# Attention with rotary rows: each causal mask one bf16 product over all 128 rows, both scores of a head pair first, in place of two on 64-row halves

## The chip, the cores and the metric

The kernel runs on one core of a Trainium2 chip. The metric is device time in microseconds (us) for one execution. It holds a whole model of four layers in one launch; the change touches one of its stages.

## The reference

Four layers of mixed attention, recurrences and experts follow one another. The stage in question is the attention of layer 3, with compressed keys and values and with rotary parts:

```python
kv_c = x @ W_kv
kv_c = kv_c * rsqrt(mean(kv_c * kv_c) + EPS) * g_kv
q_c = x @ W_q
k = concatenate([heads(kv_c @ W_kdec, 8), rope(heads(x @ W_krope, 32))])   # 16 heads, 40 rows each
q = concatenate([heads(q_c @ W_qdec, 8), rope(heads(q_c @ W_qrope, 32))])
v = heads(kv_c @ W_vdec, 8)
scores = einsum('bhqd,bhkd->bhqk', q, k) * scale
scores = where(causal, scores, -inf)
out = softmax(scores) @ v
return out_of_heads @ W_o
```

## The kernel before

A stage is a block in which each engine has its own instruction stream, with semaphores between them and a barrier at either end; no stage overlaps the next. `rotary_attention` (L666) works on 8 batches of 512 tokens. Queries and keys lie in `qs` and `ks` with tokens along the free axis: a head takes 40 rows (`KEYED`), even heads at rows 0 to 63 and odd ones at rows 64 to 127, so that two heads are two products on the two halves of the matrix array. Row 40 (`ROWS` is 41) holds, for the queries, the negated maximum of the row and, for the keys, ones.

Each batch goes through two passes. First the **maxima**: for head `n` and query tile `qt`, the scores of 128 queries against the keys up to and with that tile, 128 to 512 columns, are made by `side(("max", ...))` at L877, masked, and DVE reduces them at L1026 to a negated maximum per query (`negmax`). Even heads use bank 6 and odd heads bank 7; PE waits for `taken6` or `taken7`, which DVE signals after its reduction, before it writes a bank anew. The maxima are transposed (`turn`, L884) and sent through DRAM into row 40 of `qs`.

Then the **scores**, transposed, keys by queries: `scores(b, u, pair)` at L926 makes two heads of a pair, 41 rows, from 128 to 512 columns (`first(kt)` to 512), in banks 0 to 3, masks the diagonal tile, and ACT takes the exponential at L1004. `values(b, u)` at L942 multiplies by the values with 128 rows and 32 columns, four heads side by side.

The **mask** is added on the matrix engine: the product of an identity with a table of 0 and -1e30 is accumulated on the diagonal tile of 128 x 128 scores. `masked(out, r, kind)` (L860 to L862) does it on the half of the array that the head uses: two bf16 products of 64 rows, `j` 0 and 1, with the identity and the table split by rows into two halves that are both stored on either half of the partitions (`masksb`, 128 x 2 x 3 x 128). `kind` 1 is the mask of the maxima, 2 that of the transposed scores.

The order on PE is written out: first the maxima of batch 0, 32 pairs (`pair_of_maxima`), called the opening stretch here. Then for each batch 16 steps `u`. A step holds the scores of pair 0, a pair of maxima of the next batch, the scores of pair 1, another pair of maxima, the values of step `u - 1`, and, in some steps, extras from `extras(b, u)`: projections of the batch after the next (L886 to L903), transposes (L884), the sums and the context of the batch before (L912) and its output (L915). The last batch has no maxima to make beside it. The f32 products are two instructions each, one after the other.

The two products of a head are independent of those on the other half: in the order of the program, each pair of maxima is product and masks of the even head, then product and masks of the odd head; a pair of scores is both products, then the masks of both.

Of the kernel before, what the change touches and what calls it, by code (L numbers as in the profile page):

```python
# [14 lines left out]
F32 = mybir.dt.float32  # L15
# [650 lines left out]
def rotary_attention(nc, g, w, d):  # L666
# [7 lines left out]
    tensors = {"qs": ([P, 2, HALVES, T], F32), "ks": ([P, 2, HALVES, T], F32), "negmax": ([P, KT, NH], F32), "maxrow": ([GH, 2, T], F32), "vaug": ([P, 2, KT, NH * CELL], F32),  # L674
               "pt": ([P, 2, KT, T], F32), "o": ([P, 2, T], F32), "sel": ([P, 4, P], F32), "sums": ([P, T], F32), "nope": ([P, 2, T], F32), "prod": ([P, 2, 4, T], F32), "rope": ([P, 2, 2, T], F32),
               "wkv": ([P, 32], F32), "gkv": ([32, 1], F32), "wq": ([P, 64], F32), "wkdec": ([32, P], F32), "wqdec": ([64, P], F32), "wvdec": ([32, P], F32), "wkrope": ([P, 4, P], F32),
               "wqrope": ([64, 4, P], F32), "wo": ([P, P], F32), "cos": ([P, T], F32), "sin": ([P, T], F32), "masks": ([P, 2, 3, P], F32), "masksb": ([P, 2, 3, P], BF16),
               "kvc": ([32, 2, T], F32), "kvsq": ([32, T], F32), "qc": ([64, T], F32), "mean32": ([32, P], F32)}
    loads = [("sel", "sel")] + [(a, "L3a_" + a) for a in ("wkv", "gkv", "wq", "wkdec", "wqdec", "wvdec", "wkrope", "wqrope", "wo", "cos", "sin", "masks")]

# [28 lines left out]
    def pair_of_maxima(b, i):  # L709

        return [("max", b, 2 * (i // KT) + r, i % KT) for r in range(2)]
# [39 lines left out]
    with stage(nc, "L3a", tensors, signals) as (block, t, s):  # L751
# [80 lines left out]
        @block.gpsimd  # L832
        def _(pool):
            own = Chain(pool, s["pool"])
            own(pool.memset(t["mean32"][:, :], 1.0 / 32))
            pool.wait_ge(s["loaded"], START + LOADED)
            own(pool.tensor_copy(t["masksb"][:, :, :, :], t["masks"][:, :, :, :]))
            for r in range(2):
                own(pool.memset(t["ks"][64 * r + 32:64 * r + 64, :, :, :], 1.0))
            own(pool.memset(t["vaug"][:, :, :, :], 0.0))  # L840
            cells = t["vaug"][:, :, :, :].rearrange("p e kt (n c) -> p (e kt) n c", c=CELL)
            own(pool.memset(cells[:, :, :, 3 * HD:4 * HD], 1.0), s["pool_ready"], 1)
            for b in range(BATCH):
                for k in range(4):
                    part, half = divmod(k, 2)
                    for ab in range(2):
                        taken(pool, ("rope", b, part, half, ab))

                    pool.wait_ge(s[f"rope_written{k % 2}"], START + (2 * b + k // 2) * 16)
                    prod = t["prod"][:, k % 2, :, :]  # L850
                    pool.tensor_tensor(t["rope"][:, k % 2, 0, :], prod[:, 0, :], prod[:, 3, :], ALU.subtract).then_inc(s["rope_made"], 1)
                    pool.tensor_tensor(t["rope"][:, k % 2, 1, :], prod[:, 2, :], prod[:, 1, :], ALU.add).then_inc(s["rope_made"], 1)

        @block.tensor
        def _(pe):
            pe.wait_ge(s["loaded"], START + LOADED)
            pe.wait_ge(s["pool_ready"], START + 1)

            def masked(out, r, kind):

                for j in range(2):
                    mm = pe.matmul(out, t["masksb"][64 * r:64 * r + 64, j, 0, :], t["masksb"][64 * r:64 * r + 64, j, kind, :], start=False, stop=(j == 1))  # L862
                return mm

            def side(item):

                bank, k = place[item]
                pe.wait_ge(s[f"taken{bank}"], START + k)
                what, b = item[:2]
                out = ps[:, bank, :]  # L870
                tokens = h[:, b * T:(b + 1) * T]
                if what == "max":
                    n, qt = item[2:]
                    if n % GH == 0 and qt == 0:
                        pe.wait_ge(s["second_stacked" if n else "first_stacked"], START + (b + 1) * STACKED)
                    rows = row_tile(n % 2, KEYED)
                    pe.matmul(out[:, 0:(qt + 1) * P], t["qs"][rows, b % 2, n // 2, qt * P:(qt + 1) * P], t["ks"][rows, b % 2, n // 2, 0:(qt + 1) * P], start=True, stop=False)  # L877
                    mm = masked(out[:, qt * P:(qt + 1) * P], n % 2, 1)
                elif what == "turn":
                    k = item[2]  # L880
                    for r in range(2):
                        taken(pe, ("max", b, GH * k + GH - 2 + r, KT - 1))
                    for qt in range(KT):
                        mm = pe.transpose(out[0:GH, qt * P:(qt + 1) * P], t["negmax"][:, qt, GH * k:GH * (k + 1)], g["ident"][:, :])  # L884
                elif what == "kv":
                    mm = pe.matmul(out[0:32, :], t["wkv"][:, :], tokens, start=True, stop=True)  # L886
                elif what == "qc":
                    mm = pe.matmul(out[0:64, :], t["wq"][:, :], tokens, start=True, stop=True)
                elif what == "rms":
                    pe.wait_ge(s["squared"], START + b + 1)  # L890
                    mm = pe.matmul(out, t["mean32"][:, :], t["kvsq"][:, :], start=True, stop=True)
                elif what == "qn":
                    taken(pe, ("qc", b))
                    mm = pe.matmul(out, t["wqdec"][:, :], t["qc"][:, :], start=True, stop=True)
                elif what == "kn":
                    pe.wait_ge(s["scaled"], START + b + 1)
                    mm = pe.matmul(out, t["wkdec"][:, :], t["kvc"][:, b % 2, :], start=True, stop=True)
                elif what == "rope":
                    part, half, ab = item[2:]
                    if part:  # L900
                        mm = pe.matmul(out, t["wqrope"][:, 2 * half + ab, :], t["qc"][:, :], start=True, stop=True)
                    else:
                        mm = pe.matmul(out, t["wkrope"][:, 2 * half + ab, :], tokens, start=True, stop=True)  # L903
                elif what == "v":
                    pe.wait_ge(s["scaled"], START + b + 1)
                    for kt in range(KT):
                        cols = slice(kt * P, (kt + 1) * P)
                        mm = pe.matmul(out[:, cols], t["kvc"][:, b % 2, cols], t["wvdec"][:, :], start=True, stop=True)
                elif what in ("sums", "ctx"):
                    pe.wait_ge(s["o_copied"], START + 2 * b + 2)  # L910
                    for e in range(2):
                        mm = pe.matmul(out, t["sel"][:, (2 if what == "sums" else 0) + e, :], t["o"][:, e, :], start=(e == 0), stop=(e == 1))  # L912
                else:
                    taken(pe, ("ctx", b))
                    mm = pe.matmul(out, t["wo"][:, :], t["sums"][:, :], start=True, stop=True)  # L915
                mm.then_inc(s[f"ready{bank}"], 1)

            def scores(b, u, pair):

                four, kt = divmod(u, KT)  # L920
                step = b * NH + u
                if step:
                    pe.wait_ge(s["exp_ready"], START + 4 * (step - 1) + 2 * pair + 2)
                for r in range(2):
                    rows = row_tile(r, ROWS)
                    pe.matmul(ps[:, 2 * pair + r, first(kt):T], t["ks"][rows, b % 2, 2 * four + pair, kt * P:(kt + 1) * P], t["qs"][rows, b % 2, 2 * four + pair, first(kt):T],  # L926
                              start=True, stop=False)
                for r in range(2):
                    masked(ps[:, 2 * pair + r, kt * P:(kt + 1) * P], r, 2).then_inc(s["turned_ready"], 1)

            def values(b, u):

# [13 lines left out]
            for item in begun(0) + [("v", 0)] + begun(1):  # L946
                side(item)
            for i in range(NH * KT // 2):
                for item in pair_of_maxima(0, i):
                    side(item)  # L950
                if i == NH * KT // 4 - 1:
                    side(("turn", 0, 0))
            for b in range(BATCH):
                for u in range(NH):
                    if u % GH == 0:
                        pe.wait_ge(s["max_stacked"], START + (2 * b + u // GH + 1) * 32)
                    for pair in range(2):
                        scores(b, u, pair)
                        if b + 1 < BATCH:
                            for item in pair_of_maxima(b + 1, 2 * u + pair):  # L960
                                side(item)
                    if u:
                        values(b, u - 1)
                    for item in extras(b, u):
                        side(item)
                values(b, NH - 1)
# [2003 lines left out]
def layout(inp):  # L2970
# [59 lines left out]
    freqs = np.outer(np.arange(T, dtype=np.float32), 1.0 / 10000.0 ** (np.arange(0, 32, 2, dtype=np.float32) / 32))  # L3030
    o["L3a_cos"], o["L3a_sin"] = (np.repeat(f(freqs).T, 8, 0).astype(np.float32) for f in (np.cos, np.sin))
    later = np.where(np.arange(P)[None, :] > np.arange(P)[:, None], -1e30, 0.0)
    rows = np.stack([np.eye(P), later, later.T], 1).reshape(2, 64, 3, P).transpose(1, 0, 2, 3)
    o["L3a_masks"] = np.concatenate([rows, rows]).astype(np.float32)

    sel = np.zeros((P, 4, P), np.float32)
    for n in range(HEADS):
# [100 lines left out]
```

## Time and profile before

| | us |
|---|---|
| median of 3 executions | 9413.75 |
| lowest and highest | 9409.73, 9447.94 |
| the profiled execution | 9411.23 |
| its span, first to last instruction | 9409.6 |
| PE busy over the span | 6565.9 (70%) |
| DVE busy | 4731.6 (50%) |
| ACT busy | 3170.9 (34%) |
| POOL busy | 2124.2 (23%) |
| mean granted TensorE clock | 0.808 |

The page lists the cost of each group of instructions by its line; PE is the multiplication and PEld the loading of weights, which overlaps it. The granted clock is given as a share of 2.4 GHz: 0.50 is 1.2 GHz. Matmul records overlap, since a product starts while the one before is still draining, so what one costs is read from start to start and not from its listed length.

### The profile page before, as it was taken

The numbers are of one execution on the slowest core, as the hardware profiler recorded it, in microseconds if no ns is written. First come the engines' busy times: TensorE is split into PE (matmuls) and PEld (weight loads), VectorE is DVE, ScalarE is ACT, GpSimd is POOL, SyncE is SP. The second block draws the span as 40 slices with busy tenths as digits, with TensorE's granted clock in tenths as the row PEclk, the third lists the DMA queues.
The fourth block names the chain that finished last, engine by engine and source line by source line (L and its number), as shares of the span: only waits on it lengthen the run. The fifth ranks groups of instructions, "written<-read, shape, count | busy, mean of one in ns | idle before, by whom it ended". The sixth has DMA issues, their size and how long they took to land. (4 is left out here: it accounts for less than half of the span.)

```text
span 9409.6 us, 109969 instructions
## 1 busy us (share of the span) xinstructions
PE 6565.9 (70%) x36292; PEld 3470.7 (37%) x36480; DVE 4731.6 (50%) x7361; ACT 3170.9 (34%) x6905; POOL 2124.2 (23%) x2294
## 2 busy tenths in 40 slices
PE   5677665668766787644556999967677666667677
PEld 3666651511244122211112444434244333334343
DVE  4545534356533665677773444444444555444444
ACT  2111023225433354233331122345354333345354
POOL 1222230322133220233341100033142000043241
PEclk7888776768887788877777687889898777788898
DMA  1000010122111110000000322111110000011110
GB/s 39 0 0 0 10 56 2 66 63 63 54 47 63 43 40 14 12 0 0 0 3 12 67 47 46 23 49 37 33 38 20 7 0 0 12 41 33 36 39 26
DMA packets 260733, 267.76 MB, mean 28 GB/s; under 512 B 113312, under 2 KB 190240, under 8 KB 258400
## 3 DMA queue, kind: packets, MB, share of 16 engines
q1 hardware_dynamic: 250080, 241.23, 9.9%
q0 software_dynamic: 10240, 21.25, 0.7%
q8 instruction: 231, 3.78, 0.2%
q14 instruction: 182, 1.49, 0.1%
HBM read 123.56 MB, written 71.66 MB: 21 GB/s over the span
## 5 line engine op out<-in xcount | busy, mean ns | idle before, releaser
L2036 PE MATMUL ps<-s_l2b_hc,ident 128*128 128x512 f32 x512 | 354.3, 830 | 403.2 <-DVE s_l2b_hc L2128 402.7
L2003 POOL TENSOR_TENSOR s_l2b_Bx<-s_l2b_du,s_l2b_B 128x512 f32<-128x512 f32 x256 | 409.8, 1624 | 620.5 <-DVE s_l2b_du L2116 375.1
L1869 DVE TENSOR_REDUCE s_l3l_negmax<-ps 128x4 f32<-128x512 f32 x256 | 175.0, 683 | 743.6 <-PE ps L1710 743.6
L1710 PE MATMUL ps<-s_l3l_qk 64*64 64x64 f32 (+1 forms) x5632 | 297.6, 255 | 289.6 <-DMA s_l3l_qk<-s_l3l_rope 270.6
L2123 DVE TENSOR_TENSOR_SCAN s_l2b_state<-s_l2b_decay,s_l2b_Bx 128x512 f32<-128x512 f32 x256 | 430.7, 1721 | 109.2 <-POOL s_l2b_Bx L2003 109.2
L1800 ACT ACTIVATE s_l3l_probs<-ps,s_l3l_biases,s_l3l_q_inverse 128x128 f32<-128x128 f32 x1024 | 455.6, 463 | 54.1 <-DVE s_l3l_biases L1871 53.6
L1648 POOL TENSOR_TENSOR s_l3l_probs<-s_l3l_probs,s_l3l_inverse 128x512 f32<-128x512 f32 x256 | 266.7, 1042 | 832.7 <-DVE s_l3l_inverse L1850 832.7
L1672 PE MATMUL ps<-s_l3l_hs,s_l3l_wqk 128*128 128x512 f32 x512 | 301.2, 694 | 195.7 <-DVE s_l3l_prod L1824 100.4
L1026 DVE TENSOR_REDUCE s_L3a_negmax<-ps 128x1 f32<-128x128 f32 (+3 forms) x512 | 236.0, 488 | 350.0 <-PE ps L862 347.7
L602 DVE TENSOR_REDUCE s_L1a_negmax<-ps 128x1 f32<-128x512 f32 x512 | 316.3, 681 | 145.2 <-PE ps L464 144.5
L877 PE MATMUL ps<-s_L3a_ks,s_L3a_qs 40*128 40x256 f32 (+3 forms) x1024 | 354.4, 597 | 31.4 <-DVE s_L3a_kvsq L1041 16.5
L1004 ACT ACTIVATE s_L3a_pt<-ps 128x256 f32<-128x256 f32 (+3 forms) x512 | 195.2, 434 | 516.6 <-PE ps L862 515.0
L602 DVE TENSOR_REDUCE s_L2a_negmax<-ps 128x1 f32<-128x512 f32 x512 | 316.4, 681 | 93.2 <-PE ps L464 92.4
L1794 ACT ACTIVATE s_l3l_turned<-ps 128x512 f32<-128x512 f32 x256 | 153.5, 600 | 533.7 <-PE ps L1718 532.8
L577 ACT ACTIVATE s_L1a_pt<-ps 128x512 f32<-128x512 f32 x512 | 263.0, 602 | 205.4 <-PE ps L500 205.2
L2036 PEld LDWEIGHTS ps<-s_l2b_hc,ident 128*128 128x128 f32 x512 | 121.0, 256 | 570.7 <-DVE s_l2b_hc L2128 346.8
L577 ACT ACTIVATE s_L2a_pt<-ps 128x512 f32<-128x512 f32 x512 | 263.3, 603 | 168.2 <-PE ps L500 168.0
L1606 POOL MEMSET s_l3l_hs<- 64x2 f32 x4 | 0.4, 96 | 1301.2 <-POOLq L42 1301.2
L1710 PEld LDWEIGHTS ps<-s_l3l_qk 64*64 64x64 f32 x5632 | 230.7, 144 | 148.5 <-issue 148.5
L926 PE MATMUL ps<-s_L3a_qs,s_L3a_ks 41*128 41x512 f32 (+3 forms) x1024 | 278.8, 556 | 0.1
L1770 ACT ACTIVATE s_l3l_sq<-ps 128x512 f32<-128x512 f32 x256 | 152.2, 599 | 348.4 <-PE ps L1672 347.7
L1192 PE MATMUL ps<-s_l0a_T,s_l0a_M 128*128 128x128 f32 x1024 | 172.7, 321 | 117.7 <-DVE s_l0a_I L1319 88.4
(673 smaller groups left out, 16026.0 us busy)
## 6 DMA issues: line engine op xcount, KB each, us to landing
s_l3l_qk<-s_l3l_rope SPq DMA_DIRECT2D x1024, 64.0 KB, 2.0
scratch_rope<-s_L3a_rope SPq DMA_DIRECT2D x32, 512.0 KB, 2.8
s_L3a_qs<-scratch_rope SPq DMA_DIRECT2D x64, 128.0 KB
s_L3a_ks<-scratch_rope SPq DMA_DIRECT2D x64, 128.0 KB
s_L0e_slots<-scratch_sent SPq DMA_DIRECT2D x16, 396.0 KB, 6.8
s_L1e_slots<-scratch_sent SPq DMA_DIRECT2D x16, 396.0 KB, 6.2
scratch_square<-s_L1a_rows SPq DMA_DIRECT2D x24, 256.0 KB, 3.1
scratch_parts<-s_L1a_split SPq DMA_DIRECT2D x16, 384.0 KB, 3.1
```

What stands on the lines that cost most here:

```text
L577: act.activation(t["pt"][:, u % 2, j, :], ps[:, j, :], ACT.Exp, scale=scale).then_inc(s["exp_ready"], 1)
L602: taken_by(vec.tensor_reduce(t["negmax"][:, qt, n:n + 1], out, AX.X, ALU.max, negate=True), item)
L877: pe.matmul(out[:, 0:(qt + 1) * P], t["qs"][rows, b % 2, n // 2, qt * P:(qt + 1) * P], t["ks"][rows, b % 2, n // 2, 0:(qt + 1) * P], start ...
L926: pe.matmul(ps[:, 2 * pair + r, first(kt):T], t["ks"][rows, b % 2, 2 * four + pair, kt * P:(kt + 1) * P], t["qs"][rows, b % 2, 2 * four + ...
L1026: taken_by(vec.tensor_reduce(t["negmax"][:, qt, n:n + 1], out[:, 0:(qt + 1) * P], AX.X, ALU.max, negate=True), item)
L1648: own(pool.tensor_tensor(tile, tile, share, ALU.mult), s["probs_ready"], U + 1)
L1672: mm = pe.matmul(out, t["wqk"][:, 2 * e + ab, :], tokens, start=True, stop=True)
L1710: mm = pe.matmul(out[rows, P * k + at:P * k + at + size], t["qk"][rows, b % 2, c, 64 * m:64 * m + 64], t["qk"][rows, b % 2, 4 + c, key:key ...
L1800: act.activation(t["probs"][:, U % (LAG + 1), k, :], ps[:, U % 2, P * k:P * (k + 1)], ACT.Exp, bias=t["biases"][:, U % (LAG + 1), k:k + 1] ...
L2003: pool.tensor_tensor(t["Bx"][:, n % 2, k, :], t["du"][:, k, :], t["B"][:, n % 2, :], ALU.mult).then_inc(s["bx_ready"], 1)
L2036: pe.matmul(ps[:, 4 + k, :], g["ident"][:, :], t["hc"][:, (n - 1) % 2, k, :], start=(n == 1), stop=(n == STATES)).then_inc(s["summed"], 1)
L2123: vec.tensor_tensor_scan(t["state"][:, k, :], t["decay"][:, n % 2, k, :], t["Bx"][:, n % 2, k, :], 0.0, ALU.mult, ALU.add).then_inc(s["sca ...
```

## The change

The table is no longer split: `masksb` is 128 x 3 x 128, with identity and masks over all 128 partitions. `masked` is one bf16 product of 128 rows. The pairs of maxima leave `side` and get a function of their own, `two_maxima`, in which both waits and both products come first and the two masks after them. `scores` keeps its order, with the new masks.

```diff
-"masks": ([P, 2, 3, P], F32), "masksb": ([P, 2, 3, P], BF16),
+"masks": ([P, 3, P], F32), "masksb": ([P, 3, P], BF16),
...
-            own(pool.tensor_copy(t["masksb"][:, :, :, :], t["masks"][:, :, :, :]))
+            own(pool.tensor_copy(t["masksb"][:, :, :], t["masks"][:, :, :]))
...
-            def masked(out, r, kind):
-
-                for j in range(2):
-                    mm = pe.matmul(out, t["masksb"][64 * r:64 * r + 64, j, 0, :], t["masksb"][64 * r:64 * r + 64, j, kind, :], start=False, stop=(j == 1))
-                return mm
+            def masked(out, kind):
+
+                return pe.matmul(out, t["masksb"][:, 0, :], t["masksb"][:, kind, :], start=False, stop=True)
+
+            def two_maxima(b, i):
+
+                pair = pair_of_maxima(b, i)
+                for item in pair:
+                    n, qt = item[2:]
+                    bank, k = place[item]
+                    pe.wait_ge(s[f"taken{bank}"], START + k)
+                    if n % GH == 0 and qt == 0:
+                        pe.wait_ge(s["second_stacked" if n else "first_stacked"], START + (b + 1) * STACKED)
+                    rows = row_tile(n % 2, KEYED)
+                    pe.matmul(ps[:, bank, 0:(qt + 1) * P], t["qs"][rows, b % 2, n // 2, qt * P:(qt + 1) * P], t["ks"][rows, b % 2, n // 2, 0:(qt + 1) * P], start=True, stop=False)
+                for item in pair:
+                    qt, bank = item[3], place[item][0]
+                    masked(ps[:, bank, qt * P:(qt + 1) * P], 1).then_inc(s[f"ready{bank}"], 1)
...
-                    masked(ps[:, 2 * pair + r, kt * P:(kt + 1) * P], r, 2).then_inc(s["turned_ready"], 1)
+                    masked(ps[:, 2 * pair + r, kt * P:(kt + 1) * P], 2).then_inc(s["turned_ready"], 1)
...
-    rows = np.stack([np.eye(P), later, later.T], 1).reshape(2, 64, 3, P).transpose(1, 0, 2, 3)
-    o["L3a_masks"] = np.concatenate([rows, rows]).astype(np.float32)
+    o["L3a_masks"] = np.stack([np.eye(P), later, later.T], 1).astype(np.float32)
```

## Rows read from the trace of the kernel before

**Rows 1.** Busy us by stretch (PE, PEld, DVE, ACT, POOL), granted clock, DMA.

```profile
5215.00:5288.00 73.00, 71.21 (x259) 43.08 (x261) 31.09 (x66) 1.87 (x2) 4.92 (x4) 0.50 0.45 80
5290.00:6077.00 787.00, 752.41 (x5181) 394.85 (x5180) 338.34 (x603) 237.20 (x568) 59.76 (x48) 0.82 0.21 42
```

**Rows 2.** Waits, 5290 to 6036 us: total us, times, longest.

```profile
ACT s_L3a_pt L1004 <- PE ps L862: 497.2, 207, 35.5
...
PEld ps L877 <- DVE s_L3a_negmax L1026: 8.6, 39, 0.4
```

**Rows 3.** Groups by line: count, busy us, mean ns, idle before.

```profile
L862 PE MATMUL ps<-s_L3a_masksb 64*128 64x128 bf16 x2048 | 231.1, 245 | 0.0
...
L1026 DVE TENSOR_REDUCE s_L3a_negmax<-ps 128x1 f32<-128x128 f32 (+3 forms) x512 | 236.0, 488 | 350.0 <-PE ps L862 347.7
```

**Rows 4.** Order of time, 2.4 GHz: start us, length us, engine, line.

```profile
5615.97 0.64 PE L926 MATMUL ps<-s_L3a_qs,s_L3a_ks 41*128 41x512 f32 x1
...
5616.46 0.15 PEld L862 LDWEIGHTS ps<-s_L3a_masksb 64*128 64x128 bf16 x2 [0.19 <-issue]
5616.88 0.27 PE L862 MATMUL ps<-s_L3a_masksb 64*128 64x128 bf16 x3
...
5617.00 0.43 PE L877 MATMUL ps<-s_L3a_ks,s_L3a_qs 40*128 40x256 f32 x1
```

**Rows 5.** Order of time, 1.2 GHz, a pair of 384 columns.

```profile
5598.86 1.65 PE L877 MATMUL ps<-s_L3a_ks,s_L3a_qs 40*128 40x384 f32 x4
...
5599.61 0.21 PEld L862 LDWEIGHTS ps<-s_L3a_masksb 64*128 64x128 bf16 x2 [0.25 <-issue]
...
5600.25 0.48 PE L862 MATMUL ps<-s_L3a_masksb 64*128 64x128 bf16 x4
5600.46 1.01 PE L926 MATMUL ps<-s_L3a_qs,s_L3a_ks 41*128 41x384 f32 x2
```

**Rows 6.** Order of time on PE, 2.4 GHz, where the shape changes.

```profile
6782.54 0.27 PE L1710 MATMUL ps<-s_l3l_qk 64*64 64x128 f32 x1
6782.74 0.33 PE L1718 MATMUL ps<-ident,s_l3l_probs 128*128 128x128 f32 x1
...
5543.38 1.02 PE L912 MATMUL ps<-s_L3a_o,s_L3a_sel 128*128 128x512 f32 x2
...
5543.81 0.59 PE L912 MATMUL ps<-s_L3a_o,s_L3a_sel 128*128 128x512 f32 x1
5544.34 0.59 PE L926 MATMUL ps<-s_L3a_qs,s_L3a_ks 41*128 41x384 f32 x2
```

**Rows 7.** The same at 1.2 GHz.

```profile
6983.83 0.42 PE L1710 MATMUL ps<-s_l3l_qk 64*64 64x128 f32 x1
6984.18 0.47 PE L1718 MATMUL ps<-ident,s_l3l_probs 128*128 128x128 f32 x1
```

**Rows 8.** Weight loads after a change of shape, 512 columns, 2.4 GHz.

```profile
5614.50 0.30 PEld L926 LDWEIGHTS ps<-s_L3a_qs,s_L3a_ks 41*128 41x128 f32 x4 [0.20 <-issue]
5615.04 0.10 PEld L862 LDWEIGHTS ps<-s_L3a_masksb 64*128 64x128 bf16 x2 [0.23 <-issue]
```

**Rows 9.** A batch by stretches: masks (PE, PEld), clock; then all engines, first stretch.

```profile
5416.20:5433.30 17.10, 3.57 (x28) 2.75 (x28) 0.50 0.00 1
5433.30:5477.60 44.30, 11.32 (x106) 7.71 (x106) 1.00 0.12 43
5477.60:5498.10 20.50, 4.99 (x40) 4.06 (x40) 0.50 0.56 92
5498.10:5525.40 27.30, 8.12 (x84) 6.10 (x84) 1.00 0.40 60
...
5416.20:5433.30 17.10, 17.10 (x84) 9.58 (x81) 4.51 (x10) 2.62 (x6) 0.00 (x0) 0.50 0.00 1
```

**Rows 10.** Order of time on PE, where the clock rose and fell.

```profile
5430.33 5.15 PE L912 MATMUL ps<-s_L3a_o,s_L3a_sel 128*128 128x512 f32 x8
...
5524.67 0.95 PE L877 MATMUL ps<-s_L3a_ks,s_L3a_qs 40*128 40x384 f32 x4 [2.76 <-DVE s_L3a_kvsq L1041]
```

More of the change, by code:

```diff
@@ L676, in rotary_attention @@
                "wkv": ([P, 32], F32), "gkv": ([32, 1], F32), "wq": ([P, 64], F32), "wkdec": ([32, P], F32), "wqdec": ([64, P], F32), "wvdec": ([32, P], F32), "wkrope": ([P, 4, P], F32),
-               "wqrope": ([64, 4, P], F32), "wo": ([P, P], F32), "cos": ([P, T], F32), "sin": ([P, T], F32), "masks": ([P, 2, 3, P], F32), "masksb": ([P, 2, 3, P], BF16),
+               "wqrope": ([64, 4, P], F32), "wo": ([P, P], F32), "cos": ([P, T], F32), "sin": ([P, T], F32), "masks": ([P, 3, P], F32), "masksb": ([P, 3, P], BF16),
                "kvc": ([32, 2, T], F32), "kvsq": ([32, T], F32), "qc": ([64, T], F32), "mean32": ([32, P], F32)}
@@ L871, in side @@
                 tokens = h[:, b * T:(b + 1) * T]
[L872 to L879, printed above, removed]
+                if what == "turn":
                     k = item[2]
@@ L948, in _ @@
             for i in range(NH * KT // 2):
-                for item in pair_of_maxima(0, i):
-                    side(item)
+                two_maxima(0, i)
                 if i == NH * KT // 4 - 1:
@@ L959, in _ @@
                         if b + 1 < BATCH:
-                            for item in pair_of_maxima(b + 1, 2 * u + pair):
-                                side(item)
+                            two_maxima(b + 1, 2 * u + pair)
                     if u:
```

## The prediction, made before the changed kernel was run

> **What bounds the kernel now.** The change touches one stage only, the attention with rotary rows, so I first looked for that stage in the view by stretches. Its loop over heads runs from 5215 to 6077 us of the span: the opening stretch of 73 us, which computes only the maxima of batch 0, and then 787 us in which scores, maxima of the next batch and values go round together [rows 1]. PE is listed as busy 752 of the 787 us there. The view of waits says the same from the other side: ACT waits 497 us for the masks of the scores, whereas PE's weight loads for the maxima wait only 8.6 us for DVE's reduction [rows 2]. So the matrix engine sets the time of the stage, and what an edit adds to PE's sequence in the 787 us lengthens the kernel nearly one for one. No other stage starts before this one ends, so nothing gives it back. The opening stretch is different: there each bank's product, masks and reduction form a loop, and a latency counts.
>
> The second thing to read is the granted clock, in the same view: 0.50 in the opening stretch (1.2 GHz throughout) and 0.82 in the 787 us, a mixture of 2.4 and 1.2 GHz [rows 1].
>
> **What a mask costs today.** There are 2048 mask products at L862 [rows 3], four for each pair of heads, in 512 pairs: 256 pairs of scores and 256 of maxima. 32 of the latter are in the opening stretch and 480 pairs in the loop. The order in time at 2.4 GHz reads so: the first pass of a f32 score starts at 5615.97; its second pass starts when the weight load of the mask does, at 5616.46, 0.49 us later (0.43 is the flow of 512 columns, 0.05 a weight load that isn't hidden); the masks start at 5616.88, with no gap; the next score starts at 5617.00, so the two masks hold their half of the array for 0.12 us [rows 4]. The two heads of the pair run side by side, one on rows 0 to 63 and one on 64 to 127, a few hundredths apart, so 0.12 us is the price of all four masks. At 1.2 GHz it is 0.11 for the weight load (0.75 less 0.64 us of 384 columns) and 0.21 for the masks [rows 5].
>
> **The mask products themselves.** After the change two products of 128 rows follow one another. Each is 128 columns long like those of today: 2 x 0.055 = 0.11 us, where two of 64 rows on each half take 0.12. Halving the count from 2048 to 1024 therefore buys nothing on the path: what was done side by side is now done in series. At 1.2 GHz, 2 x 0.107 against 0.21: nothing either. The trace has no bf16 product of 128 rows in this place; from below I take no gain, from above a second mask that waits for a whole weight load of 0.10 instead of 0.055 us, 0.05 x 512 = 23 us. I take nothing, since the masks of today follow one another with the same load between them.
>
> **The change of shape is what costs.** The scores keep 40 or 41 rows on one half of the array, the masks now span both. So PE changes between a half and the whole twice per pair, where it stayed in halves. The trace shows what such a change costs between other lines. From a 64x64 to a 128x128 shape: 0.20 us from the start of a product whose flow takes 0.11, so 0.09 us is lost. From 128x128 back to a half: 5543.81 to 5544.34 is 0.53 us against 0.43 between two passes of the same shape just before, 0.10 lost [rows 6]. At 1.2 GHz: 0.35 against a flow of 0.21, 0.14 lost [rows 7]; I take 0.14 for the way back too, for which no row stands here. The weights of the second pass are hidden worse after a change: 0.54 instead of 0.49 us from the first to the second pass [rows 8]; 0.05 more, and I take the same at 1.2 GHz. Each pair thus pays 0.09 + 0.10 + 0.05 = 0.24 us at 2.4 GHz and 0.14 + 0.14 + 0.05 = 0.33 us at 1.2 GHz. The Trainium skill has the rule in "TensorEngine Tiling (Array Packing)", Key Properties: changing the tiling mode, and not only the tile, drains the engine. It speaks against this change, and by that rule the trace agrees: 0.09 to 0.10 us in each direction, none between equal shapes.
>
> How many pairs run at which clock: in 109.2 us, one batch, 68 of 258 masks fall in the two stretches at 0.50 [rows 9], 26 in 100. Of 480 pairs that is 125 slow and 355 fast: 125 x 0.33 + 355 x 0.24 = 41 + 85 = 126 us.
>
> **The opening stretch.** Both scores now come before either mask, and the masks need the whole array. Today the two banks run their loops apart: product, two masks, own reduction. Now they meet, and the loop from one pair to the next holds both reductions in a row. It gains one reduction, 0.49 us in the mean [rows 3], and a change of shape, 0.14, and loses one mask before the signal, 0.11: 0.52 us x 32 = 17 us. In the loop over heads that serialisation is covered: the next product for these banks comes only after a scores pair or the values, and the values already need both halves of the array.
>
> **Small parts.** The table of masks is half as long, so its load and the cast on GpSimd at the stage's start are shorter. They happen once, and I cost them at nothing. The waits for both banks ahead of the first mask replace waits that stood in the same order; queued behind them on PE are only the masks of the same pair. ACT and DVE get their inputs 0.1 to 0.2 us later, beside idle time that is far larger [rows 2].
>
> Sum at an unchanged clock: 126 + 17 = 143 us.
>
> **The clock.** This is the uncertain term. PE was busy all 17.1 of 17.1 us in a stretch at 0.50, so being occupied isn't what lifts the clock [rows 9]. It rose at 5433.3, while 128x128 products of 512 f32 columns ran, and fell at 5525.4, after a gap of 2.76 us in which PE waited for DVE's reciprocal [rows 10]. The other rise, at 5498.1, came with nothing but scores, maxima and values about, and opened 27.3 us at full clock with 84 masks [rows 9]. That rise looks weak: PE will do the same work there with 0.33 us more of standing per pair. I expect about half of the six such rises to be missed. One missed stretch is 27.3 + 21 x 0.24 = 32 us of work at half the clock, some 27 us more (the waits in it don't stretch): 3 x 27 = 80 us. In the Trainium skill, "TensorE: Matmul & The Clock Gate", Part 1, the clock is set by how busy PE has been. By that rule alone, with PE listed as busy throughout in both kernels, the clock would stay as it is; the first rival below is that case, and the row with 17.1 busy us at 0.50 speaks against reading the rule by listed busy time.
>
> **Forecast.** 143 + 80 = 223 us. The profiled execution took 9411.2 us (span 9409.6), 2.5 under the median of 9413.75, which is no difference here. 9411 + 223 = 9634 us.
>
> **The rivals.**
> - The tax is paid and the clock pattern stays: 9411 + 143 = 9554 us. For it: the gaps that bring the clock down are the same, and 128x128 products come in every batch. Chance 0.25.
> - The tax is paid and the clock is mostly lost in the loop: if half of the remaining 520 us at 2.4 GHz, beyond the 3 stretches, falls to 1.2 GHz, 200 us more or so, 9830 us. For it: every pair of the fast stretches gets thinner too. Against: those with projections of 128 rows in them are dense. Chance 0.12.
> - Nothing moves: the weights of the wide mask are loaded while the scores still flow, and the change of shape is free. Then 0.11 stands for 0.12 us, 9411 us within 10. Against it stand rows 6 and 7. Chance 0.04.
> - Faster: the change of shape is free and products over all 128 rows lift the clock, as they do at 5433. The 787 us at 0.82 hold 283 us at 1.2 GHz; if half of these ran at 2.4 GHz, 70 us would be saved, 9340 us. It decides only where the changes of shape cost less than what the clock gives back, 143 us or 0.14 us per change at most, and the rows put them at 0.09 to 0.14. Chance 0.03.
> - The forecast's own case has 0.56.
>
> Range: low end, the first rival without the weight-load term (0.05 x 512 = 26 us less) and a little better clock, 9535. High end, the forecast with the late second mask (23 us) and four more stretches lost (108 us), 9762, rounded to 9760. That leaves out the faster and the unmoved case and most of the lost clock, 0.2 together. A measurement of this kernel can tell about 0.5%, 47 us, from no change: slower 0.92, same 0.05, faster 0.03.
>
> **What would show it.** In the order of time: masks start 0.09 us after the end of the scores' flow, the next score 0.10 us after the end of the second mask's; 0.54 us between passes at 512 columns. The loop's granted clock under 0.80, with a stretch at 0.50 where 5498 to 5525 was fast. The opening stretch near 90 us in place of 73. The prediction is wrong if the mask's weights are fetched ahead of the change of shape, if PE stops being the bound (ACT's wait for masks would shrink far under 497 us), or if the wide masks count for more in the clock than the narrow ones did.

## The result and the profile after

The changed kernel takes 9589.5 us in the median of 4 executions (9567.8 to 9623.8); the kernel before takes 9421.1 in executions on the same chip. The ratio is 1.0178, with a 95% interval of 1.014 to 1.0216: slower by 168 us. The profiled execution, the shortest of the four, took 9567.8 us with a span of 9566.0, 156 us over the span of before. In all comparisons here two executions are left out in which the chip granted far less clock from start to end: 11514.6 us of the kernel before and 11712.6 us of one of the variants below.

First the view by stretches, the one that says where the time went. Each row gives the stretch, its length, busy us of PE, PEld, DVE, ACT and POOL, the granted clock and the DMA. In this and all such fences the first row is the opening stretch, from the first product of the maxima to the first score, and the second row the loop over heads, to the last score. The kernel before, cut at the same events, then its two last batches (these rows are cut more finely than rows 1):

```profile
5215.10:5287.60 72.50, 70.78 (x259) 42.65 (x260) 30.80 (x64) 1.87 (x2) 4.92 (x4) 0.50 0.45 80
5287.60:6076.90 789.30, 754.71 (x5189) 396.53 (x5187) 339.73 (x605) 237.13 (x567) 59.76 (x48) 0.82 0.21 42
5962.70:6036.60 73.90, 71.53 (x672) 41.59 (x668) 34.77 (x70) 26.14 (x67) 0.00 (x0) 1.00 0.12 17
6036.60:6076.90 40.30, 40.16 (x380) 18.92 (x378) 5.54 (x5) 24.00 (x62) 0.00 (x0) 1.00 0.01 2
```

The changed kernel:

```profile
5200.90:5286.80 85.90, 70.18 (x196) 32.42 (x196) 28.33 (x64) 1.87 (x2) 4.92 (x4) 0.50 0.37 68
5286.80:6235.10 948.30, 919.71 (x4227) 341.99 (x4228) 335.52 (x605) 237.94 (x568) 59.69 (x48) 0.73 0.18 34
6105.20:6189.60 84.40, 82.13 (x542) 34.05 (x538) 33.96 (x69) 26.14 (x67) 0.00 (x0) 1.00 0.10 12
6189.60:6235.10 45.50, 45.45 (x319) 17.27 (x316) 5.93 (x6) 24.81 (x63) 0.00 (x0) 1.00 0.01 2
```

The loop is 159 us longer, the opening stretch 13. The stages ahead came out 12 us shorter in this one execution, which no line of the change explains, and 4 us more went at the start of this stage, where the table of masks is now shorter, and behind it. Of the 159 us, read the clock column: 0.82 became 0.73. A loop of 789.3 us at 0.82 holds 647 us of work at 2.4 GHz, one of 948.3 at 0.73 holds 692. So the work grew by about 45 us, and the time at 1.2 GHz went from 2 x 0.18 x 789 = 284 us to 2 x 0.27 x 948 = 512. This product undercounts the added work: waits and changes of shape in a slow stretch are not twice as long, and more of them now lie in slow stretches. The last two batches ran at 1.00 in both kernels and show the added work with no clock in it: 10.5 us and 5.2 us. Seven batches like the first and one like the second would make 7 x 10.5 + 5.2 = 79 us (an estimate).

Next the order of time on PE in the changed kernel, at 2.4 GHz and then at 1.2 GHz, to be held against rows 4 and 5 (start us, length us, engine, line):

```profile
5710.04 0.28 PE L932 MATMUL ps<-s_L3a_qs,s_L3a_ks 41*128 41x128 f32 x2
5710.25 0.29 PE L861 MATMUL ps<-s_L3a_masksb 128*128 128x128 bf16 x2
5710.46 0.92 PE L873 MATMUL ps<-s_L3a_ks,s_L3a_qs 40*128 40x384 f32 x4
5711.31 0.29 PE L861 MATMUL ps<-s_L3a_masksb 128*128 128x128 bf16 x2
...
5701.33 0.39 PE L861 MATMUL ps<-s_L3a_masksb 128*128 128x128 bf16 x2
5701.40 0.31 PE L861 MATMUL ps<-s_L3a_masksb 128*128 128x128 bf16 x1
5701.65 2.08 PE L873 MATMUL ps<-s_L3a_ks,s_L3a_qs 40*128 40x512 f32 x4
5703.66 0.39 PE L861 MATMUL ps<-s_L3a_masksb 128*128 128x128 bf16 x2
```

The second pass of a score starts at 5710.04 and flows for 0.11 us (128 columns); the masks start at 5710.25, so 0.10 is lost. From the first mask to the next score it is 0.21: two masks one after the other, 0.12, and 0.10 for the way back. From 5710.46 to 5711.31 it is 0.85: two flows of 0.32, 0.11 for the second pass's weights and 0.10 again. At 1.2 GHz it is 0.32 us from the first mask to the next score. The second mask starts at 5701.40 (the row with x1 is the second of the two in the row above it), so 0.25 us lies between its start and the score; its flow takes 0.11, which leaves 0.14 for the change. The 2.01 us from 5701.65 to 5703.66 hold two flows of 0.85, 0.16 for the weights and 0.14 for the change.

The count, as the view of groups has it, against rows 3, and the wait of ACT against rows 2 (here over 5286.8 to 6107 us):

```profile
L861 PE MATMUL ps<-s_L3a_masksb 128*128 128x128 bf16 x1024 | 172.0, 260 | 0.0
...
ACT s_L3a_pt L1008 <- PE ps L861: 586.7, 186, 41.9
```

Half as many masks, as meant. ACT waits longer for PE, so PE is still the bound. And the clock, against rows 9: three of the stretches at 1.2 GHz (masks of PE and PEld, clock) are 44 to 55 us long, where those of rows 9 were 17 and 20. Such a stretch isn't new, since the loop of the kernel before has one of 47.8 us as well; but it has only that one over 40 us, where the changed kernel has four of 44 to 58 us. The last rows show one place of the difference: steps 14 and 15 of a batch and steps 0 and 1 of the next, first in the kernel before (all engines, at full clock and in the one case that it missed wholly), then in the changed one.

```profile
5385.00:5439.60 54.60, 10.65 (x54) 3.55 (x54) 0.50 0.41 59
5531.70:5586.30 54.60, 10.24 (x52) 3.42 (x52) 0.50 0.41 59
5661.40:5705.80 44.40, 7.10 (x36) 2.37 (x36) 0.50 0.30 54
...
5606.20:5625.20 19.00, 18.80 (x173) 10.70 (x170) 8.68 (x19) 6.71 (x17) 0.00 (x0) 0.97 0.53 71
5715.20:5746.10 30.90, 30.90 (x172) 16.17 (x168) 8.63 (x19) 6.71 (x17) 0.00 (x0) 0.54 0.31 44
...
5705.90:5727.20 21.30, 20.97 (x141) 8.27 (x138) 8.58 (x19) 6.71 (x17) 0.00 (x0) 1.00 0.50 63
5553.60:5588.40 34.80, 34.80 (x142) 11.88 (x138) 8.70 (x19) 6.71 (x17) 0.00 (x0) 0.53 0.30 39
```

Of the six passages from one batch to the next that stand in these two traces, the kernel before went through one wholly and one in part at 1.2 GHz; in the changed kernel it was three wholly, at 34 to 36 us each in place of 21.3, and one in part.

### The profile page after: what moved, and what is told of

The parts are those of the page before. It is cut to its first block and busy times, and to the rows that moved or that the text cites. A ratio compares the mean times of both kernels' runs of the same rounds, so it can differ in the third digit from the quotient of the medians.

```text
span 9566.0 us, 107921 instructions
## 1 busy us (share of the span) xinstructions
PE 6717.1 (70%) x35268; PEld 3403.3 (36%) x35456; DVE 4724.2 (49%) x7361; ACT 3171.9 (33%) x6905; POOL 2128.3 (22%) x2294
## 5 line engine op out<-in xcount | busy, mean ns | idle before, releaser
L873 PE MATMUL ps<-s_L3a_ks,s_L3a_qs 40*128 40x128 f32 (+3 forms) x1024 | 340.4, 669 | 36.0 <-DVE s_L3a_kvsq L1045 15.9
```

What stands on the lines that cost most here:

```text
L873: pe.matmul(ps[:, bank, 0:(qt + 1) * P], t["qs"][rows, b % 2, n // 2, qt * P:(qt + 1) * P], t["ks"][rows, b % 2, n // 2, 0:(qt + 1) * P], ...
```

## The experiments

Three questions: is it the change of shape or the new order that costs (A against B); is the lower clock brought by the thinner work on the array (D against E); and can the clock be had back. Ratios are against the kernel before, timed beside them.

**The order alone.** `two_maxima` with the old masks on halves:

```diff
-                    masked(ps[:, bank, qt * P:(qt + 1) * P], 1)...
+                    masked_half(ps[:, bank, qt * P:(qt + 1) * P], item[2] % 2, 1)...
...
-                    masked(ps[:, 2 * pair + r, kt * P:(kt + 1) * P], 2)...
+                    masked_half(ps[:, 2 * pair + r, kt * P:(kt + 1) * P], r, 2)...
```

> The order of the changed kernel (both products of a pair of maxima, then the masks) with the masks of the old one, two products of 64 rows on each head's half. Theory A (changes of shape cost the time): PE never leaves the halves here, so the loop over heads stays at 789 us within 10 and the opening stretch at 72 us; total 9421 us within 25. Theory B (the two heads wait for each other, whatever the mask's shape): the loop keeps over half of the 159 us that the changed kernel added, 870 us or more, total 9500 us or more. The clock of the loop stays at 0.82 by A.

Measured 9443.6 us in the median, ratio 1.0027 (1.0011 to 1.0042). Stretches:

```profile
5224.50:5303.30 78.80, 65.89 (x258) 42.50 (x260) 28.26 (x64) 1.87 (x2) 4.93 (x4) 0.50 0.40 73
5303.30:6123.70 820.40, 778.36 (x5192) 391.07 (x5189) 334.85 (x605) 237.20 (x568) 59.75 (x48) 0.80 0.20 40
```

Theory A is right in the main, since 1.0027 is a small part of 1.0178, but its "unchanged" was wrong. The order costs 6.3 us in the opening stretch, nearly half of the 13.4 there, and in the profiled execution (9455.3 us, 12 over the median) 31 us in the loop, where the clock was 0.80. Theory B's half of the loss is not there.

**Wide masks for the scores alone, and for the maxima alone**, each with masks on halves for the other, whose table is loaded and cast beside the wide one before the opening stretch:

```diff
-                    masked(ps[:, bank, qt * P:(qt + 1) * P], 1)...                    # scores alone
+                    masked_half(ps[:, bank, qt * P:(qt + 1) * P], item[2] % 2, 1)...
...
-                    masked(ps[:, 2 * pair + r, kt * P:(kt + 1) * P], 2)...            # maxima alone
+                    masked_half(ps[:, 2 * pair + r, kt * P:(kt + 1) * P], r, 2)...
```

> Masks of 128 rows for the scores, masks on halves for the maxima (in the new order). Theory A: a step has 6 changes of shape where the old kernel has 2 (into and out of each scores' mask, beside those around the values) and 2 more passes whose weights are exposed: 4 x 0.095 + 2 x 0.05 = 0.48 us per step, 112 steps, plus 0.335 us in the 16 steps of the last batch: 59 us on the loop at 2.4 GHz, some 65 with the part at 1.2 GHz, and up to 40 more if the clock falls; opening stretch unchanged at 72 us. Total 9485 to 9525. Theory B: no change against the old kernel beyond 15 us.

Measured 9594.4 us, ratio 1.0168 (1.0124 to 1.0213).

```profile
5216.40:5295.20 78.80, 65.90 (x258) 42.52 (x260) 28.26 (x64) 1.87 (x2) 4.93 (x4) 0.50 0.38 73
5295.20:6258.80 963.60, 934.45 (x4680) 395.34 (x4677) 335.86 (x605) 237.87 (x568) 59.76 (x48) 0.69 0.18 34
```

> Masks of 128 rows for the maxima, masks on halves for the scores. Theory A: 5 changes of shape per step where the old kernel has 2, one more exposed pass: 3 x 0.095 + 0.05 = 0.335 us x 112 = 38 us on the loop, 45 with the part at 1.2 GHz, none in the last batch, and the opening stretch goes from 72 to 85 us as in the changed kernel. Total 9465 to 9510. Theory B: most of what the changed kernel lost is here, over 100 us, and little in the kernel with wide masks for the scores alone.

Measured 9509.6 us in the median of three executions (9507.5 to 9559.5), ratio 1.012 (1.0072 to 1.0167).

```profile
5210.30:5296.20 85.90, 70.23 (x198) 32.47 (x198) 28.30 (x65) 1.87 (x2) 4.92 (x4) 0.50 0.37 67
5296.20:6182.50 886.30, 850.45 (x4737) 367.46 (x4738) 335.28 (x605) 237.25 (x567) 59.71 (x48) 0.76 0.19 37
```

The opening stretch follows the shape of the maxima's masks, as A said, but from another start: 78.8 us with the order alone and with wide masks for the scores (A had 72), 85.9 with wide masks for the maxima, as in the changed kernel. So its 13.4 us are 6.3 for the order and 7.1 for the shape. The loops miss: both are longer than A's sum, by some 110 and some 50 us, and of the totals that of the wide scores lies outside A's range, while that of the wide maxima is at its upper end. The two halves of the change are not additive either, 1.0168 and 1.012 against 1.0178 together. The clock column shows why. With wide scores alone the loop ran at 0.69, lower than with both, so a loop with less added work (963.6 x 0.69 = 665 us at full clock) took more time. Of its 174 us over the old loop A's count explains some 65, and the rest is left for the clock. So what the clock does isn't a fixed price for each change of shape.

**Fewer changes of shape.** The changed kernel with the masks of a scores pair held back behind the products of the maxima pair:

```diff
                     pe.matmul(ps[:, bank, 0:(qt + 1) * P], t["qs"][...], t["ks"][...], start=True, stop=False)
+                between()
                 for item in pair:
...
-                            two_maxima(b + 1, 2 * u + pair)
+                            two_maxima(b + 1, 2 * u + pair, lambda: score_masks(b, u, pair))
```

> The changed kernel with the masks of a scores pair held back until the two products of the maxima pair behind it are issued, then all four wide masks in a row: 5 changes of shape per step instead of 9, same products and masks. Theory A: 4 x 0.095 + 2 x 0.05 = 0.48 us per step less than the changed kernel, 54 us at 2.4 GHz and about 60 with the slow part, and some of the lost clock back: loop 948 down to 830 to 890 us, clock 0.75 to 0.80, total 9480 to 9545. Theory C (the wide masks themselves hold the array up or draw the clock down, not the changes): the loop stays over 920 us.

Measured 9533.1 us, ratio 1.0118 (1.0089 to 1.0146).

```profile
5231.40:5317.50 86.10, 70.19 (x197) 32.43 (x197) 28.44 (x64) 1.87 (x2) 4.93 (x4) 0.50 0.37 67
5317.50:6211.00 893.50, 851.30 (x4229) 380.38 (x4228) 334.75 (x605) 237.99 (x569) 59.66 (x48) 0.76 0.19 37
```

The same wide masks, 5 changes of shape per step in place of 9: the loop is 55 us shorter (893.5, just over A's 830 to 890), and the clock is 0.76, within what A said. C is out: the wide masks are all there.

**Does density hold the clock?** Three kernels are meant to change only how much dense work there is: the old one with every mask added twice, the changed one with every mask added three times (adding the mask again leaves the result as it is), and the old one without masks, in which the products give the signals that the masks gave, and whose attention isn't causal inside the diagonal tile.

```diff
-                for j in range(2):
+                for j in range(2 * 2):       # halves, twice; j % 2 picks the table
...
-                return pe.matmul(out, ..., start=False, stop=True)
+                for again in range(3):       # wide, three times
+                    mm = pe.matmul(out, ..., start=False, stop=(again == 2))
...
-                    mm = pe.matmul(out, t["masksb"][...], t["masksb"][...], start=False, stop=(j == 1))
+                return None                  # no masks
```

> The old kernel with each mask on a half added twice, eight products per pair where it has four, order and everything else unchanged. It adds 0.115 us per pair at 2.4 GHz, with no change of shape and no gap: 480 x 0.115 = 55 us on the loop over heads (789 us at a clock of 0.82, that is 648 us of work at full clock). Theory D (the clock follows how much of the array is at work, and the masks, which fill both halves with one column per cycle, are dense work): the clock rises to 0.88 or more and the loop comes to (648 + 55) / 0.90 = 780 us, 760 to 815, no longer than before. Theory E (the clock goes its own way and only gaps move it): the clock stays at 0.82 and the loop comes to 855 us or more; total 9490.

Measured 9519.5 us, ratio 1.0101 (1.0075 to 1.0127).

```profile
5310.70:6209.70 899.00, 874.25 (x7107) 473.05 (x7106) 355.91 (x604) 238.83 (x568) 59.67 (x48) 0.86 0.19 37
```

> The changed kernel with each wide mask added three times in a row: 3072 wide products instead of 1024, the changes of shape as many as in the changed kernel. It adds 4 x 0.055 = 0.22 us per pair, 480 x 0.22 = 105 us at full clock to 696 us of such work in the loop. Theory D (dense work lifts the clock): the clock goes from 0.73 to 0.88 or more and the loop to (696 + 105) / 0.90 = 890 us, shorter than the 948 of the changed kernel although it does more. Theory E: the clock stays at 0.73 and the loop is 1050 us or more, total 9690.

Measured 9569.5 us, ratio 1.0165 (1.0143 to 1.0187).

```profile
5301.20:6239.30 938.10, 912.68 (x6145) 433.05 (x6144) 335.52 (x605) 239.04 (x569) 59.68 (x48) 0.86 0.18 35
```

> The old kernel with the masks left out, of the maxima and of the scores, so that attention is not causal inside the diagonal tile; everything else as before. It takes 0.115 us of the densest work from each pair: 55 us off the loop's 648 us of work at full clock. Theory E (the clock doesn't follow the density): clock 0.82, loop 725 us, opening stretch 66, total 9345. Theory D: the clock falls, to 0.70 to 0.76, and eats the gain or more: loop 593 / 0.73 = 810 us, 780 to 850; total 9400 to 9470.

Measured 9420.1 us, ratio 1.0007 (0.9994 to 1.002).

```profile
5283.30:6083.00 799.70, 760.21 (x3271) 330.88 (x3269) 340.89 (x605) 238.73 (x567) 59.75 (x48) 0.72 0.21 41
```

This is the clearest result of the study. With no masks at all the loop is 10 us longer than with 2048 of them, and the kernel as a whole takes the same time; the work at full clock fell from 647 to 799.7 x 0.72 = 576 us, and the clock gave all of it away. The changed kernel with three times its wide masks did 807 us of work in place of 692 and its profiled loop took 10 us less, though over all executions the two kernels can't be told apart (1.0165 and 1.0178). Theory D had the clock about right in advance (0.88 or more against 0.86, 0.70 to 0.76 against 0.72), but gave the tripled masks too much, a loop of 890 us where 938 was measured. E is out, and not by one execution alone: the mean clock over the whole program was 0.811 to 0.816 in every execution with doubled masks and 0.811 to 0.814 with tripled ones, 0.804 to 0.810 in the kernel before, 0.794 to 0.800 in the changed one and 0.795 to 0.802 without masks. PE is listed as busy for 95 to 97% of all these loops, whether the clock was 0.72 or 0.86. What these runs show is that mask products added or left out move the clock; which property of them does it (rows, columns or their type) they don't separate.

The old kernel with its masks doubled got D's clock too, 0.86, but its loop is 899 us, not 760 to 815: its work at full clock is 773 us, 126 more than before where I had worked out 55. The order of time at the maxima (PE, then DVE) shows something that I hadn't counted:

```profile
6050.49 1.07 PE L878 MATMUL ps<-s_L3a_ks,s_L3a_qs 40*128 40x512 f32 x2
6051.41 0.22 PE L863 MATMUL ps<-s_L3a_masksb 64*128 64x128 bf16 x1
6051.41 0.69 PE L878 MATMUL ps<-s_L3a_ks,s_L3a_qs 40*128 40x512 f32 x1
...
6050.36 0.56 DVE L1027 TENSOR_REDUCE s_L3a_negmax<-ps 128x1 f32<-128x384 f32 x1 [0.64 <-PE ps L863]
```

The second head's product at 6051.41 starts with the first head's first mask, 0.92 us after the first head's product. DVE had left the bank at 6050.92. In the old kernel, where two masks lie between the two heads in the program's order and not four, both heads can run side by side: in rows 5 the four passes of a pair of maxima are over in 1.65 us [rows 5]. They don't always do so there, since a bank is often handed back late: the first passes of the two heads start within 0.1 us of each other in 100 of the old kernel's 256 pairs of maxima. With all masks doubled it is none. So doubling the masks of the maxima took the two heads apart; that this makes up all of the 71 us is argued, not shown. It also suggests what the new order of the changed kernel is good for: it puts the two products next to each other.

**Can the clock be had back?** The clock falls after PE's gap of 2.76 us for DVE's reciprocal [rows 10], which comes once in each of six batches. Four kernels built on the old one:

```diff
-                    act.activation(t["kvsq"][:, :], ..., ACT.Sqrt, ...).then_inc(s["rooted"], 1)         # early bank
+                    act.activation(t["kvsq"][:, :], ..., ACT.Sqrt, ...).then_inc(s[f"taken{place[item][0]}"], 1)
...
-                    vec.wait_ge(s["rooted"], START + b + 1)
-                    taken_by(vec.reciprocal(t["kvsq"][:, :], t["kvsq"][:, :]), item)
                     taken(vec, item)
+                    vec.reciprocal(t["kvsq"][:, :], t["kvsq"][:, :]).then_inc(s["rooted"], 1)
+                    vec.wait_ge(s["rooted"], START + b + 1)
...
-        if u in (1, 2, 5) and nxt:                                                       # moved
+        if u in (1, 3, 5) and nxt:      # and ahead of it, in step 3, the values ("v")
...
-                    masked(ps[:, 2 * pair + r, kt * P:(kt + 1) * P], r, 2)...            # scores twice
+                    masked(ps[:, 2 * pair + r, kt * P:(kt + 1) * P], r, 2, 2)...
```

> The old kernel, with bank 6 handed back by ACT's square root, which is the last to read it, instead of by DVE's reciprocal of 3.34 us that follows (the two semaphores change places). PE's gap of 2.76 us before the maxima of step 3, after which the clock falls in every batch, should shrink to 1 to 1.6 us, since 1.6 us of products stand between. Theory D1 (the fall comes from this gap): the 17 us at 1.2 GHz after it go in most of the six batches, loop 789 down to 735 to 765 us, clock 0.86 to 0.90. Theory D2 (what is left of the gap, or the thin work around it, still brings the clock down): loop 780 to 790, only the gap's own 1.5 us x 6 saved.

Measured 9436.2 us, ratio 1.0024 (1.0013 to 1.0034).

```profile
5279.60:6101.90 822.30, 794.73 (x5191) 414.13 (x5189) 339.50 (x605) 236.52 (x568) 59.81 (x48) 0.77 0.21 40
...
5410.72 3.34 DVE L1041 RECIPROCAL s_L3a_kvsq<-s_L3a_kvsq 32x512 f32<-32x512 f32 x1 [1.98 <-ACT s_L3a_kvsq L989]
...
5412.85 0.27 PE L862 MATMUL ps<-s_L3a_masksb 64*128 64x128 bf16 x2
5415.36 1.69 PE L877 MATMUL ps<-s_L3a_ks,s_L3a_qs 40*128 40x512 f32 x2 [2.23 <-DVE s_L3a_negmax L1026]
```

A miss. PE got its bank early, ran the next pair and then stood for 2.23 us at the one after, because DVE was in the reciprocal until 5414.06 and had its own product and the reductions still to do; the clock was 0.77. The gap only moved by one pair. Neither D1's loop of 735 to 765 us nor D2's of 780 to 790 came; why the clock fell below that of the old kernel isn't shown.

> The old kernel with the masks of the scores added twice, those of the maxima once. 256 pairs x 0.115 = 29 us more work at full clock in the loop: 648 + 29 = 677 us. Theory D (dense work holds the clock): 0.87 to 0.90 in place of 0.82, loop 752 to 778 us, shorter than the 789 of the old kernel. Rival (the work added outweighs what the clock gives): clock 0.83 to 0.85, loop 800 to 815 us. In the kernel with all masks doubled the second head of a maxima pair started 0.43 us after the first instead of beside it; here it should start beside it again, as in the old kernel.

Measured 9411.2 us, ratio 0.9993 (0.9979 to 1.0008).

```profile
5286.50:6093.80 807.30, 777.33 (x6210) 419.63 (x6208) 337.77 (x605) 238.08 (x567) 59.73 (x48) 0.83 0.21 41
```

The rival's numbers (0.83, 807 us); over all executions no difference. The two heads of a pair of maxima start side by side again, within 0.1 us in 130 of 256 pairs, as was expected with two masks between them (the 0.43 us of the expectation is 0.92 in the rows with all masks doubled).

> Bank 6 handed back early and the scores' masks added twice. Theory D: both reasons for a low clock are met, 0.93 or more, loop 677 / 0.93 = 728 us, total about 9360. Rival: no better than the better of the two alone.

Measured 9386.9 us, ratio 0.9963 (0.9949 to 0.9977).

```profile
5283.80:6062.70 778.90, 749.44 (x6211) 408.51 (x6208) 337.22 (x605) 237.69 (x568) 59.77 (x48) 0.86 0.21 42
```

Better than either alone, but 28 us of the 55 or so that D promised, and a clock of 0.86 in place of 0.93.

> Bank 6 handed back early, and the step that makes the root mean square moved from u = 2 to u = 3, so that the long scores of 512 columns of step 4 lie behind it instead of the short ones of 128 columns. PE then has over 2 us of products while DVE takes the reciprocal. Theory D1: the gap of 2.76 us is gone, and with it the stretch of 17 us at 1.2 GHz in each of six batches: loop 730 to 755 us, total 9350 to 9380. Rival: DVE's two reciprocals of 3.3 us, for the root and for the sums, now fall into one step, PE waits for the second instead, and the loop stays at 780 to 795 us.

Measured 9364.4 us, ratio 0.9946 (0.993 to 0.9963).

```profile
5281.20:6036.80 755.60, 733.82 (x5191) 382.72 (x5189) 339.46 (x605) 237.19 (x567) 59.74 (x48) 0.84 0.22 43
...
5413.50:5427.10 13.60, 13.54 (x48) 6.29 (x49) 5.24 (x7) 4.73 (x7) 0.00 (x0) 0.50 0.06 20
...
5413.56 2.07 PE L891 MATMUL ps<-s_L3a_kvsq,s_L3a_mean 32*128 32x512 f32 x2 [0.78 <-DVE s_L3a_vaug L1057]
```

The long scores of step 4 cover the reciprocal. Of the gap a wait of 0.78 us for DVE's copy of the values is left, and the loop is 34 us shorter than the old one at the same products, 1 us outside D1's range. D1's reason holds only in part: the stretch at 1.2 GHz that was to go is still there, 13.6 us in place of 17.1 (second row). Besides the gap itself the loop gained by evenness: batches 1 to 5 took 105.8 to 105.9 us each, where the old kernel's took 109 to 124, with slow stretches that differ from batch to batch; whether the early bank or the moved step did this wasn't run apart.

> The kernel with bank 6 handed back early and the root moved to step 3 (loop 756 us at a clock of 0.845, 638 us of work at full clock), with the scores' masks added twice besides: 29 us more work. Theory D: the stretches of 20.5 and 13.7 us at 1.2 GHz that are left in each batch thin out, clock 0.91 or more, loop 667 / 0.92 = 725 us, total 9335 to 9355. Rival (what is left of the slow stretches doesn't depend on the density of a step but on the walk through the extras): clock 0.86 to 0.88, loop 757 to 775 us, total 9365 to 9385, no gain over the kernel without the doubled masks.

Measured 9369.8 us, ratio 0.994 (0.9921 to 0.996).

```profile
5290.00:6033.90 743.90, 721.40 (x6212) 392.53 (x6208) 336.86 (x605) 238.16 (x567) 59.74 (x48) 0.90 0.22 44
```

Between the two expectations in the profile: the clock rose to 0.90 and the loop came to 744 us. The total is the rival's: over all executions it can't be told from the kernel without the doubled masks. These last two beat both kernels of the case, by 50 us against the old one; they do it with masks on halves.

## Why the prediction was right, and where its sizes were off

The forecast was 9634 us in a range of 9535 to 9760, slower with 0.92; 9589.5 was measured. The total alone doesn't tell the forecast from its first rival (9554 us, the clock unchanged), which it missed by 36 us against 45; the loop's clock of 0.73 does. The low end of the range isn't what its sum gives, 9554 - 26 = 9528, which a better clock would lower and not raise. By its steps:

- **The mask products cost nothing more or less on the path.** Right: two in a row take 0.12 us from the start of the first to the end of the second's flow, as the four of before did.
- **A change of shape costs 0.09 to 0.10 us at 2.4 GHz and 0.14 at 1.2.** Right in each direction and at both clocks, 0.10 and 0.14, the way back at 1.2 GHz too, for which a value had been assumed. The exposed weights of the second pass are 0.11 and 0.16, also as taken. The Trainium skill's rule that a change of mode drains the array ("TensorEngine Tiling (Array Packing)", Key Properties) agrees with this for bf16 products of 128 rows between f32 ones on halves.
- **126 us for 480 pairs.** Too large, by a miscount. I charged two changes and one exposed pass to each of the four pairs in a step. The old kernel already changes shape twice per step, around the values, so the pair ahead of them pays one change, not two, and the first scores already have their weights exposed. A step pays 7 changes and 3 passes more, 7 x 0.095 + 3 x 0.05 = 0.815 us in place of 4 x 0.24 = 0.96; in the last batch 3 and 1, 0.335. The last two batches, both at full clock, test it: 16 x 0.815 = 13.0 us, measured 10.5; 16 x 0.335 = 5.4, measured 5.2. In the first of these, 2.5 us went under waits that were there before (argued, not shown). Over the loop the term is about 100 us rather than 126.
- **17 us in the opening stretch.** 13.4 measured, but near by luck, since both parts were off. The meeting of the two heads was to cost a whole reduction, 0.49 x 32 = 16 us, and cost 6.3 (the order alone); why so little isn't shown. The shape was to cost 0.14 - 0.11 us a pair, 1 us in all, and cost 7.1. That is what two changes and the exposed weights less one mask come to, (0.33 - 0.11) x 32 = 7.0 us (an estimate); the prediction had charged one change there.
- **80 us for the clock.** The sign was right. The size, taken as what the loop gained beyond the count above, is 159 less about 100, some 60 us (80 if the added work is put at the 79 us that the last two batches suggest). The working behind it was right in part: the weak rise between two batches, expected to be lost three times, was lost wholly three times in the profiled execution, against once before. But a lost one took 34 to 36 us in place of 21.3, some 14 us more and not 27, so the two that came on top make up less than half of the term. The rest lies in slow steps elsewhere that the prediction didn't name, and that the total of this term came near is luck to that degree. It also moves between executions (9567.8 to 9623.8 us), and the wide scores alone lost more of it than the whole change.
- **The rule on busy time.** The first rival was the case of the Trainium skill's rule that the clock is set by how busy PE has been ("TensorE: Matmul & The Clock Gate", Part 1). Read by PE's listed busy time, the runs deny it: 760 of 800 us busy at 0.72 without masks, 913 of 938 at 0.86 with three times as many. What moved the clock there was the mask products in that time.
- **Faster.** That rival needed wide products to lift the clock by more than the changes cost. In the changed kernel the clock fell instead. Three times as many wide masks did lift it, to 0.86, and the kernel was still 1.65% slower than before.

What stays open: which property of the mask products the clock goes by, and why a given execution regains the clock in one batch and not in the next. The order of steps decides it in detail, and the study moved it in both directions without being able to say beforehand where it would land.

## What to carry to other kernels

Before you join two products on parts of the array into one on the whole, count the changes of shape that the sequence makes, at 0.10 us each here, and count those that it makes already. Products that run side by side on two halves cost no more than one wide one, so halving their number saves nothing. Where the granted clock is well under 1 while PE is listed as busy, the time of an edit isn't its count of microseconds: leaving out all the masks was worth nothing here, and handing a bank back early together with moving the step of its reciprocal ahead of long products was worth 50 us.

## What was not expected of the hardware

- Leaving out 2048 mask products changed the kernel's time by 0.07% (0.9994 to 1.002), with the loop's clock down from 0.82 to 0.72.
- With four masks of one head ahead of it in the order of the program, the other head's product, on the other half of the array and with its bank free since 6050.92, did not start before 6051.41; with two ahead the two heads of rows 5 ran side by side [rows 5]. Of 256 pairs of maxima none started within 0.1 us of each other with four masks ahead, and 100 did with two. How PE comes to this the runs don't show.
- At 1.2 GHz two wide masks in a row start 0.08 us apart (0.078 before the rounding of the rows at 5701.33 and 5701.40) and not 0.11. From the first mask to the next score 0.32 us went, of which 0.14 is the change of shape.
